# One DMA transpose of two fp16 planes in place of four fp32 TensorE transposes

## The reference

```python
def attn(x):                                   # after a layer norm of x
    qkv = x_low1 @ w1 (fp16) + x_mid @ w_mid (fp32) + x_low2 @ w2 (fp16)
    q, k, v = split(qkv); s = softmax(q / 16 @ k.T)
    return (s @ v) @ out_w.T + out_b
def ffn(x):                                    # after a layer norm of x
    x_prev = x shifted by one position of the sequence (zeros at its start)
    xr = mu_r * x + (1 - mu_r) * x_prev
    xk = mu_k * x + (1 - mu_k) * x_prev
    return sigmoid(xr @ W_r) * (square(relu(xk @ W_k)) @ W_v)
x = x + layernorm(attn(layernorm(x)))          # "residual"
x = x + layernorm(ffn(layernorm(x)))
```

## Time and profile before

| | |
|---|---|
| median of 3 runs | 847.64 us (847.51 to 848.23) |
| the profiled execution's own time | 845.67 us |
| its span in the profile | 843.9 us |
| TensorE busy | 796.9 us, 94% of the span |
| VectorE busy | 704.0 us, 83% |
| ScalarE busy | 516.9 us, 61% |
| GpSimd busy | 420.9 us, 50% |
| DMA, queue of SyncE | 100.56 MB, 56.7% of 16 engines' span |

### The profile page before, as it was taken

How to read it: one execution, slowest core, us unless ns; L and a number is a source line. 1 busy time by engine, 2 the same in 40 slices (tenths; PEclk the granted TensorE clock), 3 DMA queues, 4 the chain that set the end, 5 groups by cost and what they waited for, 6 DMA issues and landing times.

```text
span 843.9 us, 16183 instructions
## 1 busy us (share of the span) xinstructions
PE 796.9 (94%) x5873; PEld 582.2 (69%) x5873; DVE 704.0 (83%) x1808; ACT 516.9 (61%) x639; POOL 420.9 (50%) x651
## 2 busy tenths in 40 slices
PE   4779999999999999999999999999999999999953
PEld 2436677777777777777777777777777777777842
DVE  5678898987998998988898998988787787888683
ACT  3266665665676766666676666666666655667542
POOL 2020255555545565555446555654456555545872
PEclk9979999999999999999999999999999999999998
DMA  7557866557556775796445767575435455554301
GB/s 180 113 124 156 158 138 132 107 126 150 123 114 107 153 143 125 120 144 143 108 113 107 169 128 142 125 126 119 97 87 119 101 125 125 117 110 106 83 12 38
DMA packets 336575, 101.59 MB, mean 120 GB/s; under 512 B 310256, under 2 KB 336240, under 8 KB 336496
## 3 DMA queue, kind: packets, MB, share of 16 engines
q1 hardware_dynamic: 336496, 100.56, 56.7%
HBM read 18.75 MB, written 8.39 MB: 32 GB/s over the span
## 4 chain that ended last, share of the span: by engine, by line
PE 87%; DVE 7%; POOL 2%; issue 2%; ACT 1%; DMA 1%; SPq 1%; ACTq 0%; POOLq 0%; DVEq 0%
PE S L1038 6%; PE S L1040 6%; PE S L1039 6%; PE S L1042 6%; PE S L1041 6%; PE Y L1060 6%; PE Y L1062 6%; PE Y L1063 6%; PE Y L1061 6%; PE Y L1059 6%; PE M L1006 6%; PE M L1007 6%; PE M L1008 6%; PE M L1090 2%; PE M L1022 1%
## 5 line engine op out<-in xcount | busy, mean ns | idle before, releaser
L793 DVE TENSOR_SCALAR_CACHE_REDUCE probs<-S 128x512 f32<-128x512 f32 x256 | 173.0, 679 | 78.3 <-PE S L1042 74.9
L597 ACT ACTIVATE probs<-probs,exp_bias,kappa 128x2048 f32<-128x2048 f32 x64 | 134.0, 2094 | 68.2 <-DVE exp_bias L804 68.2
L809 DVE TENSOR_TENSOR p_lo<-probs,p_hi 128x2048 f16<-128x2048 f32 x64 | 162.5, 2539 | 1.9 <-ACT p_hi L547 1.9
L1059 PE MATMUL Y<-pt_hi,planes 128*128 128x256 f16 x512 | 139.7, 273 | 0.5 <-issue 0.5
L1060 PE MATMUL Y<-pt_lo,planes 128*128 128x256 f16 x512 | 139.7, 273 | 0.0
L1061 PE MATMUL Y<-pt_hi,planes 128*128 128x256 f16 x512 | 139.7, 273 | 0.0
L1063 PE MATMUL Y<-pt_hi,planes 128*128 128x256 f16 x512 | 139.7, 273 | 0.0
L1062 PE MATMUL Y<-pt_lo,planes 128*128 128x256 f16 x512 | 139.7, 273 | 0.0
L547 ACT ACTIVATE p_hi<-probs 128x2048 f16<-128x2048 f32 x64 | 121.9, 1905 | 1.1
L1038 PE MATMUL S<-turned,q_hi 128*128 128x512 f16 x256 | 98.7, 386 | 3.1 <-DVE q_lo L784 3.1
L615 ACT ACTIVATE att<-att,ashift,arstd 128x256 f32<-128x256 f32 x62 | 33.9, 593 | 107.4 <-POOL ashift L455 107.4
(11 more groups left out here) (179 smaller groups left out, 1941.0 us busy)
## 6 DMA issues: line engine op xcount, KB each, us to landing
x_res<-in_L_attn_x SPq DMA_DIRECT2D x32, 256.0 KB, 3.7
out_x<-gate SPq DMA_DIRECT2D x32, 256.0 KB, 3.1
xs<-in_L_attn_x SPq DMA_DIRECT2D x28, 128.0 KB, 3.3
xs<-in_L_attn_x SPq DMA_DIRECT2D x14, 256.0 KB, 4.1
pt_hi<-p_hi SPq DMA_TRANSPOSE x64, 4.5
pt_lo<-p_lo SPq DMA_TRANSPOSE x64, 3.7
pt_hi<-in_L_attn_weight_qkv SPq DMA_DIRECT2D x3, 128.0 KB, 3.1
pt_hi<-in_L_attn_weight_qkv SPq DMA_DIRECT2D x1, 256.0 KB, 3.2
```

What stands on the lines that cost most here:

```text
L793: dve.tensor_scalar(probs[:, t, c * BLK:(c + 1) * BLK], S[k % RING][:, :], 1.0, None, ALU.mult, ALU.max, accum_out=chunk_max[:, t, c:c + 1 ...
L809: dve.tensor_tensor(p_lo[:, t, :], probs[:, t, :], p_hi[:, t, :], ALU.subtract).then_inc(p_lo_made, 1)
L1059: pe.matmul(to[:, 0, :], low, p_h, start=first, stop=False, skip_group_check=True)
```

## The change

The normalised residual is no longer turned by TensorE, but for the last half. After `mix_in` ScalarE converts it to an fp16 plane (`mix_high`, offset 32), GpSimd subtracts it for the low plane (`mix_low`, 33), SyncE issues one DMA transpose of both planes, 128 x 1024 fp16 (`turn_mix`, 34), and GpSimd adds the two turned planes into `xt` (`mix_in_sum`, 37). The difference and the carry move from 33 to 37, both mixes from 36 and 37 to 38. The factor `mix_scale`, which ScalarE's copy applied, goes into the root of `res_rsqrt`: the variance is multiplied by `mix_shrink`, so that `rrstd` holds it. The last half keeps `turn_mix_in`, ScalarE's copy and VectorE's difference, at 33.

```diff
-    DIFF = 33
-    MIX = (36, 37)
+    MIX_HIGH = 32
+    MIX_LOW = 33
+    TURN_MIX = 34
+    DIFF = 37
+    MIX = (38, 38)
...
+        mx = sb("mx", [P, 2, RT, HALVES, P], F16)
+        mxt = sb("mxt", [P, 2, RT, HALVES, P], F16)
...
+            def turn_mix(h):
+                if h >= 1:
+                    sp.wait_ge(xt_made, h)
+                sp.wait_ge(mix_hi_made, h + 1)
+                sp.wait_ge(mix_lo_made, h + 1)
+                sp.dma_start_transpose(mxt.rearrange("p l t e r -> p (l t e) r"),
+                                       mx.rearrange("p l t e d -> p (l t e d)")).then_inc(mix_in, 16)
...
             for k in range(SLOTS):
+                if (h := at(k, TURN_MIX)) is not None and h < DRAIN:
+                    turn_mix(h)
                 for t in range(RT):
...
-                pool.tensor_tensor(rvar[:, :], rmv[:, :, 1], eps[:, :], ALU.add).then_inc(r_eps_added, 1)
+                if h == 0:
+                    pool.wait_ge(scales_made, 3 + RT)
+                pool.tensor_scalar(rvar[:, :], rmv[:, :, 1], EPS, mix_shrink[:, 1:2], ALU.add, ALU.mult).then_inc(r_eps_added, 1)
...
+            def mix_low(h):
+                if h >= 1:
+                    pool.wait_ge(mix_in, 16 * h)
+                pool.wait_ge(mix_hi_made, h + 1)
+                pool.tensor_tensor(mx[:, 1], att[:, h % 2].rearrange("p t (e d) -> p t e d", e=HALVES), mx[:, 0],
+                                   ALU.subtract).then_inc(mix_lo_made, 1)
+
+            def mix_in_sum(h):
+                pool.wait_ge(mix_in, 16 * (h + 1))
+                if h >= 2:
+                    pool.wait_ge(mixed_made, (h - 1) * 4)
+                    pool.wait_ge(carried, h)
+                pool.tensor_tensor(xt[:, h % 2, :, 1:ROWS + 1].rearrange("p e (t r) -> p t e r", t=RT), mxt[:, 0], mxt[:, 1],
+                                   ALU.add).then_inc(xt_made, 1)
...
                 if (h := at(k, RESIDUAL)) is not None and h < DRAIN:
                     add_attention(h)
+                if (h := at(k, MIX_LOW)) is not None and h < DRAIN:
+                    mix_low(h)
                 if (h := at(k, DIFF)) is not None:
                     if h < DRAIN:
+                        mix_in_sum(h)
                         differences(h)
                     carry(h)
...
+            def mix_high(h):
+                act.wait_ge(mix_in_made, (h + 1) * RT)
+                if h >= 1:
+                    act.wait_ge(mix_in, 16 * h)
+                copy(mx[:, 0], att[:, h % 2].rearrange("p t (e d) -> p t e d", e=HALVES)).then_inc(mix_hi_made, 1)
...
-                if (h := at(k, XT)) is not None:
+                if (h := at(k, MIX_HIGH)) is not None and h < DRAIN:
+                    mix_high(h)
+                if (h := at(k, XT)) is not None and h >= DRAIN:
                     mix_in_out(h)
...
-                if (h := at(k, DIFF)) is not None and h >= DRAIN:
+                if (h := at(k, XT)) is not None and h >= DRAIN:
                     differences(h)
...
-                if (h := at(k, TURN)) is not None:
-                    turn_mix_in(h, k)
+                if (h := at(k, TURN)) is not None and h >= DRAIN:
+                    turn_mix_in(h)
...
                 if (h := at(k, QUERY)) is not None and h >= 1:
                     pe.wait_ge(q_lo_made, h)
-                    if (turned_before := begun(k, TURN)) > 0:
-                        pe.wait_ge(xt_made, turned_before)
```

More of the change, by code:

```diff
@@ L136, in sandwich @@
         rec_scale = sb("rec_scale", [P, 1])
-        mix_scale = sb("mix_scale", [P, 1])
+        mix_shrink = sb("mix_shrink", [P, 2])
         feed_scale = sb("feed_scale", [P, 2])
@@ L260, in sandwich @@
         inv_top_made = sem("inv_top_made"); weight_scale_made = sem("weight_scale_made")
-        row_square_made = sem("row_square_made"); inv_row_made = sem("inv_row_made"); parts_made = sem("parts_made")
+        row_square_made = sem("row_square_made"); inv_row_made = sem("inv_row_made"); mix_part_made = sem("mix_part_made"); parts_made = sem("parts_made")
         scales_made = sem("scales_made"); feed_part_made = sem("feed_part_made"); sum_inverted = sem("sum_inverted")
@@ L281, in sandwich @@
         r_rstd_made = sem("r_rstd_made"); mix_in_made = sem("mix_in_made")
+        mix_hi_made = sem("mix_hi_made"); mix_lo_made = sem("mix_lo_made"); mix_in = sem("mix_in")
         mix_in_turned = sem("mix_in_turned"); xt_made = sem("xt_made"); carried = sem("carried")
@@ L422, in scales @@
                 pool.wait_ge(inv_top_made, 1)
-                pool.tensor_scalar(mix_scale[:, :], inv_top[:, MU:MU + 1], 2.0 ** MIX_EXP, 0.0, ALU.mult,
-                                   ALU.add).then_inc(scales_made, 1)
+                pool.tensor_scalar(mix_shrink[:, 0:1], top[:, MU:MU + 1], 2.0 ** -MIX_EXP, 0.0, ALU.mult,
+                                   ALU.add).then_inc(mix_part_made, 1)
+                pool.wait_ge(mix_part_made, 1)
+                pool.tensor_tensor(mix_shrink[:, 1:2], mix_shrink[:, 0:1], mix_shrink[:, 0:1], ALU.mult).then_inc(scales_made, 1)
                 pool.tensor_tensor(rec_part[:, :], top[:, REC:REC + 1], top[:, MU:MU + 1], ALU.mult).then_inc(parts_made, 1)
@@ L616, in attention_norm @@
                                    scale=arstd[:, t:t + 1]).then_inc(att_normed, 1)
-            def mix_in_out(h):
[L619 to L626, removed]
+            def mix_high(h):
[3 more added lines that the diff above has]
+                copy(mx[:, 0], att[:, h % 2].rearrange("p t (e d) -> p t e d", e=HALVES)).then_inc(mix_hi_made, 1)
+            def mix_in_out(h):
+                act.wait_ge(mix_in_turned, 1)
+                act.wait_ge(mixed_made, (h - 1) * 4)
+                act.wait_ge(carried, h)
+                copy(xt[:, h % 2, :, 1:ROWS + 1], pair(TURN_BANK[:, :])).then_inc(xt_made, 1)
             def split_high(h):
@@ L1083, in project_out, with turn_mix_in @@
                 by_rows(OUT_BANK, y_hi, y_lo, OUT, o_done)
-            def turn_mix_in(h, k):
+            def turn_mix_in(h):
                 pe.wait_ge(mix_in_made, (h + 1) * RT)
-                pe.wait_ge(q_lo_made, begun(k, QUERY))
+                pe.wait_ge(q_lo_made, H)
                 for e in range(HALVES):
```

## The result

The changed kernel takes 870.9 us (median, 869.5 to 872.1), against 847.6: ratio 1.0285 (95% interval 1.0264 to 1.0306), slower. The forecast was 868.5 (846 to 898). The profiled execution took 872.0 us, its span is 870.1 against 843.9, 26.2 more.

What follows compares the result with a forecast made beforehand. TensorE set the 24.14 us period; after the change a circle of in-order engines would. 17.0+2.5-3.0+7.0-2.75 = +20.8 us on the profiled 845.67 gave 866.5, 868.5 for the median; 8-in-10 range 846 to 898.

Steps and rivals of the forecast that it cites:

- The transposes' 0.43 us: On TensorE, removing four transposes saves 0.43 us a half, 31 x 0.43 = 13.3 us if nothing else becomes the bound.
- the circle: In-order waits among VectorE, ScalarE and GpSimd within one period: 14.5+5.33+2.2+1.64 = 23.7 us, a lower bound of the period.
- rival A: TensorE stays the bound throughout because the circle has unseen slack: 847.64-13.3 = 834 us; chance 0.17.
- The new path costs nothing: ScalarE's conversion, GpSimd's low plane and the DMA transpose are hidden before GpSimd's sum at c7+19.8: cost nothing.
- Preparation: Preparing the next batch lengthens the circle: eight periods 201.6 us against 193.1, 8.5 more; two such batches 17.0.
- The tail: From 775 on, without scores, mixes end at 791.0 instead of 788.7: 2.3 us for halves 28 to 30, 7.0.
- What covers some of it, once: Key matmuls start 2.75 us after `att` is made, so VectorE can fall that far behind before TensorE feels it: -2.75 us.
- rival B: On GpSimd `arstd` loses the race with p_lo and takes 2.75 us; 0.8 us in 23 periods, +18: 887; chance 0.17.
- Rival C: GpSimd's root of the residual stands in front of the mixes: 0.70 us in 27 periods, +19: 887; chance 0.05.

Runs made afterwards that it cites:

- e2: The changed kernel with sum and difference moved to 35, ahead of squares_low, and the mixes to 36 and 37, all added work kept: 842.0 us.
- e8: The e2 kernel with TensorE still making the four fp32 transposes of each half, into the bank, unread: 852.8 us.
- e7: The changed kernel with TensorE still making the four fp32 transposes of each half, into the bank, unread: 875.2 us.
- e4: The changed kernel with only the planes' sum moved to 35, difference left at 37 and mixes at 38: 847.5 us.
- e5: The changed kernel with one more GpSimd operation of the sum's size in slot 5, ahead of the sum, result unread: 907.0 us.
- e3: The changed kernel with sum and difference moved to 35, mixes left at 38, all added work kept: 842.0 us.
- e1: The kernel before with only the slots moved, difference to 37 and both mixes to 38, TensorE's transposes kept: 851.8 us.
- e6: The changed kernel with the statistics of the groups in slot 6 put ahead of the mixes instead of behind them: 864.9 us.
- e9: The e2 kernel with the path by DMA for halves 0 to 27 only, the old way for 28 to 31: 834.3 us.

## Why the prediction was right, and where it was not

- The mechanism was the one forecast, and 870.9 lies 2.4 us from the 868.5. That nearness is in part luck. On the profiled executions the sum gave 866.5 and 872.0 was measured, 5.5 us off. I had added 2.0 us because the profiled execution of the kernel before was that much under its median; the one of the kernel after was 1.1 above its own.
- The transposes' 0.43 us: right in size, shown by e2 (0.44 us a period) and e8. They do not help where the circle sets the period (e7). Their 13.3 us counted four halves too many, but the sum did not use that figure; rival A did.
- The new path costs nothing: right while scores last (e2, e8). Conversion 0.63, low plane 1.16, landing 5.4 at worst, with 4 us to spare before the sum.
- The circle: right to 0.02 us in its sum. Shown from four sides: one operation less (e4), one more (e5), opened in full (e2, e3), built into the old kernel (e1).
- Preparation: 201.6 forecast, 201.4 and 201.6 measured. Between copies of slot 7 the split differs from my list, since slot 6's statistics belong to the period before: 25.5; 26.1 and 25.4; 25.5; 26.5 and 25.0; twice 23.7. 26.1+25.4 = 51.5, where I had 24.3+27.4 = 51.7. That the eight add up to 0.2 us is thus better than the single terms were. e6 shows that its place decides.
- The tail: 7.0 forecast, 8.5 measured, and not for the forecast's reason alone. Counted from the last copy, the mixes of halves 28, 29 and 30 end 2.4, 4.9 and 5.9 us later than before. So the longer way is 5.9 us, 2.4 and 2.5 in two halves but only 1.0 in the third. The remaining 2.6 are matmuls at TensorE's lower clock, which the forecast did not have; the two errors partly cancel. Chain of the kernel before, then of the kernel after, at the last half's receptance and key matmuls (start, us, line):

```profile
818.51 0.21 PE M L1006
...
821.87 0.12 PE M L1008
```

```profile
842.03 0.21 PE M L1048
...
846.93 0.21 PE M L1050
```

  24 matmuls take 5.1 us instead of 3.5, and the next twelve 2.8 instead of 1.5: 2.9 us. Between 833 and 847 the granted clock was 0.51, that is 1.2 GHz for nearly all of it. The kernel before ran the first eight of its 24 at the lower clock as well, and the other 16 at full. That it would not have fallen without the longer waits is argued, not shown.
- "What covers some of it, once", -2.75 us: this step failed. Added up over all periods and the tail, VectorE's delay is 26.2 us, the whole difference of the spans, so nothing was covered. What TensorE can do ahead does not matter, because the tail starts from VectorE's copies. VectorE could only catch up if the circle were shorter than TensorE's period, as in e1; here both are 23.7 us. With that term at zero the sum would have been +23.5, and 871.1. The 2.7 us beyond are 1.5 in the tail, 0.9 in the last batch, 0.5 in the first, less 0.2 in the second. In the last batch the eighth period, which my list left out, makes 0.6 of it: it was 23.05 us before and is 23.69 now. Where TensorE is the bound the last period is shorter (22.61 in e2 as well), where the circle is, it is not.
- The race of rival B was won in all 29 halves whose turn comes while scores last, most often by 0.12 us: `arstd` at 750.85, p_lo at 750.97. Once both began within 0.01 us (679.83), and `arstd` still took 0.70. In the tail it was lost once by the operation ahead of the root: `avar`, 0.19 us elsewhere, started at 797.21, behind a p_lo of 796.53, and took 2.24. Rival C is refuted: four mixes took 1.68 us with a root of 0.76 us beside them. The Trainium skill's rule (SBUF — State Buffer, section "SBUF: two separate sides") that the port pair is held for a whole instruction fits the long operations of the earlier trace rows, and `avar`, which ended with p_lo. It does not fit these roots on two columns, which did not hold VectorE though they had started.

## What to carry to other kernels

When work moves to another slot, list for each engine what stands ahead of it in its order and what that waits for; if the chain comes back to the engine that waits, its length is the period's lower bound, and no busy share shows it. Add it up from rows, with whatever else stands in it now and then. The cure here was the order, not less work: two slots earlier, ahead of the operation that waits, the same added work was free while scores last. In the tail, where nothing hides the longer way, keeping the old one for the last four halves gave the fastest kernel of all (e9).

## Seen on the way

TensorE's clock also fell in the middle of the changed kernel, behind gaps, but not behind each. TensorE waited 2.35 us for `att` before 280.06 and again before 481.43, and from 279.8 to 283.8 the granted clock was 0.57, with 3.4 us at 1.2 GHz; behind the second it was 0.57 too. It stayed at 1.00 behind gaps as long or longer: 2.36 us before 558.41, and 2.70 before 357.42 (1.00 from 354 to 364). In stretches where TensorE had no gap, as in the earlier trace rows, the clock was 1.00. So the length of a single gap did not decide. In e6 a gap of 2.22 us had a fall behind it in one batch and none in the other, and the periods concerned differ by 1.1 us. The stretch behind the first gap (length, busy, granted clock, DMA share, GB/s):

```profile
279.80:283.80 4.00, 3.74 (x20) 0.57 0.72 64
```
